# Two-layer graph network on one core: 96-row node tiles, x loads at the head of layer 1, node maximum from PSUM in two banks

## The reference

```python
def _leaky(x): return jnp.where(x >= 0, x, 0.01 * x)

def _edge_conv(x, src, dst, W1, b1, W2, b2):
    x_i, x_j = x[dst], x[src]
    h = jnp.concatenate([x_i, x_j - x_i], axis=-1)
    m = _leaky(h @ W1 + b1) @ W2 + b2
    return jax.ops.segment_sum(m, dst, num_segments=50000)

h = jnp.maximum(_layernorm(x), 0.0)
for l in range(2):
    h = _edge_conv(h, src, dst, W1[l], b1[l], W2[l], b2[l])
    h = _leaky(_layer_norm(h, g[l], b[l]))
return x + h
```

## Time and profile before

| | us |
|---|---|
| median of 3 runs | 1081.89 (1065.54 to 1090.26) |
| the profiled execution, its own time | 1051.49 |
| its span, first to last instruction | 1049.8 |
| DVE busy | 816.5 |
| PE busy | 848.6 |
| POOL busy | 727.7 |
| ACT busy | 591.7 |

### The profile page before, as it was taken

The page is one execution under the profiler, slowest core; times in us unless marked ns, Lnnn a source line. Parts: engine busy times, 40 slices in busy tenths (PEclk is TensorE's granted clock), DMA queues, the critical chain, the costliest instruction groups (busy, mean ns, idle before and its releaser), DMA issues.

```text
span 1049.8 us, 21951 instructions
## 1 busy us (share of the span) xinstructions
PE 848.6 (81%) x5756; PEld 691.8 (66%) x5756; DVE 816.5 (78%) x2330; ACT 591.7 (56%) x1632; POOL 727.7 (69%) x705
## 2 busy tenths in 40 slices
PE   1577788898889898988998647998888888888864
PEld 1345676777777677766777545777777777777753
DVE  6675687787887788787876313799999999999984
ACT  0145787888888788887888410433434343343431
POOL 4877777777777777777730007788888888888544
PEclk9998899999999999999999855999999999999965
DMA  1232477888687778776875551699999999999996
GB/s 38 77 81 76 109 173 190 210 201 212 182 211 190 203 193 214 193 203 179 199 183 133 145 151 49 149 246 276 272 272 265 270 270 259 276 267 266 256 265 174
DMA packets 338395, 204.11 MB, mean 194 GB/s; under 512 B 32986, under 2 KB 322589, under 8 KB 338269
## 3 DMA queue, kind: packets, MB, share of 16 engines
q1 hardware_dynamic: 190397, 99.95, 38.6%
q10 hardware_dynamic: 129056, 64.16, 22.2%
q0 software_dynamic: 18816, 38.57, 14.2%
HBM read 124.92 MB, written 77.62 MB: 193 GB/s over the span
## 4 chain that ended last, share of the span: by engine, by line
POOL 32%; DVE 23%; issue 21%; PE 8%; DMA 7%; ACT 4%; SPq 3%; DVEq 0%; ACTq 0%; POOLq 0%
POOL e_x L583 18%; POOL e_x L576 14%; DVE e_hT L856 5%; DVE e_n L856 5%; PE psum L902 3%; DVE e_same L750 3%; DMA e_x<-in_x,src_cols 3%; DVE e_rows L866 3%; DVE e_hidT L877 2%; SPq L531 2%; DMA b_rows<-e_rows 2%; DVE w_rel L735 1%; DMA h_rows<-w_out 1%; ACT e_n L633 1%; DVE n_stats L799 1%
## 5 line engine op out<-in xcount | busy, mean ns | idle before, releaser
L583 POOL DMA_INDIRECT e_x<-h_rows,src_cols x196 | 197.4, 1007 | 148.0 <-DMA h_rows<-w_out 93.9
L902 PE MATMUL psum<-w_win,w_oh 113*128 113x128 f32 x1568 | 227.0, 291 | 36.0 <-ACT w_out L613 21.7
L583 POOL DMA_INDIRECT e_x<-in_x,src_cols x196 | 205.9, 1051 | 59.8 <-issue 59.5
L576 POOL DMA_INDIRECT e_x<-in_x,dst_idx x196 | 194.2, 991 | 73.1 <-issue 58.2
L902 PEld LDWEIGHTS psum<-w_win,w_oh 113*128 113x128 f32 x1568 | 206.9, 205 | 42.2 <-issue 31.5
L618 ACT ACTIVATE e_v<-psum 128x512 f32<-128x512 f32 x98 | 59.4, 606 | 218.2 <-DVE e_hT L856 96.7
L910 PE MATMUL psum<-e_same,e_m 128*128 128x136 f32 (+2 forms) x1168 | 169.7, 290 | 0.0
L910 PEld LDWEIGHTS psum<-e_same,e_m 128*128 128x128 f32 x1168 | 149.3, 197 | 23.2 <-issue 21.2
L738 DVE TENSOR_TENSOR w_oh<-node_iota,w_rel 112x512 f32<-112x512 f32 x196 | 142.1, 725 | 6.7
L799 DVE BATCH_NORM_STATS2 n_stats<-e_x 128x6 f32<-128x128 f32 x392 | 80.4, 278 | 70.2 <-DMA e_x<-in_x,src_cols 69.1
L633 ACT ACTIVATE e_n<-e_x,n_shift,n_inv 128x128 f32<-128x128 f32 x196 | 80.5, 490 | 0.7 <-DVE n_shift L833 0.5
(11 more groups left out here) (164 smaller groups left out, 1677.9 us busy)
## 6 DMA issues: line engine op xcount, KB each, us to landing
w_win<-b_rows SPq DMA_DIRECT2D x784, 56.4 KB
h_rows<-w_out SPq DMA_DIRECT2D x98, 256.0 KB
e_line<-dst_lines SPq DMA_DIRECT2D x49, 288.0 KB
b_rows<-e_rows SPq DMA_DIRECT2D x49, 258.0 KB
b_rows<-e_rows ACTq DMA_DIRECT2D x49, 258.0 KB
e_x<-in_x ACTq DMA_DIRECT2D x49, 256.0 KB, 5.0
out<-e_x ACTq DMA_DIRECT2D x49, 256.0 KB
w_out<-in_x ACTq DMA_DIRECT2D x36, 256.0 KB, 4.8
```

Source lines behind the costliest of these rows:

```text
L576: pool.indirect_dma_start(e_x[:, slot, 0, k, :], None, table, bass.IndirectOffsetOnAxis(dst_idx[:, g * K + k:g * K + k + 1], 0)).then_inc( ...
L583: pool.indirect_dma_start(e_x[:, slot, 1, k, :], None, table, bass.IndirectOffsetOnAxis(src_cols[:, g * K + k:g * K + k + 1], 0)).then_inc ...
L902: last = nc.tensor.matmul(b_p[:, j, :], w_oh[0:W + 1, w % RH, j, :], w_win[0:W + 1, w % RW, j, 0:D], start=True, stop=True)
```

## The change

There are four edits. `W` becomes 96. The placements of layer 1 go into two banks in turn, `b_p` and `b_f` (`b_f` was used in layer 0 only), and wait for the maximum of the window before the last (`nodes_made`) and no longer for ACT's copy of the last one. ACT multiplies by the slope as it copies, and DVE takes the maximum of the PSUM bank and this copy. The first eight x loads are issued before step 0 of layer 1, and no longer in its steps 7 to 10.

```diff
-W = 112
+W = 96
@@
+        def place_bank(l, w):
+
+            return b_f if l == 1 and w % 2 == 1 else b_p
@@ raise_nodes (ACT)
-                nc.scalar.activation(e_v[:, w % 2, :], flat(b_p), ACT.Copy).then_inc(nodes_sloped, 1)
+                nc.scalar.activation(e_v[:, w % 2, :], flat(place_bank(1, w)), ACT.Copy, scale=SLOPE).then_inc(nodes_sloped, 1)
@@ layer 1 of ACT
+            for w in range(RQ):
+                load_x(w)
             for s in range(STEPS[1] + 1):
...
                 for w in windows(s - R1 - 3):
-                    load_x(w)
+                    if w >= RQ:
+                        load_x(w)
@@ leaky_nodes (DVE)
-                p_all = e_v[:, w % 2, :].rearrange("p (k d) -> p k d", k=K)
-                nc.vector.scalar_tensor_tensor(t_ring[w % RT], p_all, SLOPE, p_all, ALU.mult, ALU.max).then_inc(nodes_made, 1)
+                nc.vector.tensor_tensor(t_ring[w % RT], place_bank(1, w)[:, :, :], e_v[:, w % 2, :].rearrange("p (k d) -> p k d", k=K),
+                                        ALU.max).then_inc(nodes_made, 1)
@@ place (PE)
                 else:
-                    need(pe, nodes_sloped, w)
+                    pe.wait_ge(nodes_made, NODE_GROUPS + max(w - 1, 0))
                     if w == 0:
-                        pe.wait_ge(nodes_made, NODE_GROUPS)
+                        pe.wait_ge(rows_made[0], GROUPS)
+                        pe.wait_ge(scaled, GROUPS)
                         pe.wait_ge(const_out, 32)
                 for j in range(K):
-                    last = nc.tensor.matmul(b_p[:, j, :], w_oh[0:W + 1, w % RH, j, :], w_win[0:W + 1, w % RW, j, 0:D], start=True,
+                    last = nc.tensor.matmul(place_bank(l, w)[:, j, :], w_oh[0:W + 1, w % RH, j, :], w_win[0:W + 1, w % RW, j, 0:D], start=True,
                                             stop=True)
```

## The result

| | before | after |
|---|---|---|
| median of 20 runs on one chip, us | 1065.6 (1044.7 to 1090.3) | 1076.9 (1058.4 to 1093.7) |
| ratio, 95% interval | | 1.0179 [1.0129, 1.0229] |
| the profiled execution, us | 1051.5 | 1059.8 |

The changed kernel is slower by 1.8%. I had forecast 0.7% faster, so the sign is wrong. The ratio compares undisturbed runs only, which for a kernel with four or six runs can be a few long ones; over all 20 runs the medians lie 1.1% apart.

What follows compares the result with a forecast made beforehand. POOL was taken to limit layer 1's steady part (7.62 of a 7.65 us step). Terms -2 - 2.5 - 3.5 + 1 - 0.5 = -7.5 us gave 1044 against the profiled 1051.5, or 1074 for the median; range 1066 to 1081, with rivals and spread 1050 to 1094.

Steps and rivals of the forecast that it cites:

- The steady part: Layer 1's 37 steps up to the last gathers: POOL stays the limit, 2 us gained; ends 11 gained and 22 lost.
- 0.05 of the 0.30: First gather of each steady step: of its 0.30 us stretch, 0.05 was expected to go, 2 us in all.
- The mechanism of the stretch: POOL's gathers: one that begins while a DVE instruction with two SBUF operands runs takes 1.24 us, not 0.94.
- The base: Steady part of layer 1: the kernel before takes 7.65 us a step, read from one profile.
- The new wait: PE's placement waiting for DVE's maximum: closes a loop of 7.0 us, below POOL's 7.62, so costed at nothing.
- After the last gather: End of layer 1: 2.5 us saved as maxima stop waiting behind adds, 3.5 saved in the last windows.
- my 4.95: Last windows of layer 1: two windows take about 4.95 us in place of 5.65, saving 3.5 us in all.
- The x loads: Between layer 0's last store and POOL's first gather: early loads delay it by 1 us, between 0 and 4.
- W (-0.5): Window transfers carry 1/7 less: 0.5 us saved where layer ends wait for windows; ends 0 and 4.
- a gain in layer 0: Sign of being wrong: layer 0 getting faster; no size given.
- The rival of the DMA limit: Steady part: DMA engines were the limit, so fewer bytes save 0.24 us a step, 9 in all; chance 0.05.
- The slower rival: Steady part: the new wait's loop, with L862 behind one POOL add, becomes 8.25 us a step, +22 us; chance 0.10.

Runs made afterwards that it cites:

- e8: Kernel before with the node numbers that L738 compares copied to a free PSUM bank, leaving it one SBUF operand; 1081.1 us, ratio 1.0162.
- e2: e1 with the placement again waiting for ACT's copy, so two banks, W = 96 and early x loads stay on the changed kernel; 1072.0 us.
- e3: Kernel before with W = 96 in place of 112 alone; 1071.9 us, ratio 1.0025.
- e4: Kernel before with the eight x loads issued ahead of layer 1 alone; 1081.8 us, ratio 1.0315.
- second profile of before: Kernel before, unchanged, run and profiled again; 1076.3 us, ratio 1.0011.
- e15: Kernel before with 17 extra products on PE at the head of layer 1; 1084.5 us, ratio 1.0297.
- e17: e15 with one push: in one step of 49, POOL's adds wait for DVE's maxima of the next pair of windows; 1065.2 us, ratio 1.0050.
- e1: Changed kernel with the old maximum, taken on DVE from the SBUF copy; 1086.8 us.
- second profile of after: Changed kernel, unchanged, run and profiled again; 1078.0 us, ratio 1.013.
- e11: Changed kernel with the first eight x loads back in steps 7 to 10; 1067.5 us, ratio 1.0142.
- e9: Changed kernel with PE's first placement of a step moved behind the message product and ACT's copy of it behind the squares; 1087.3 us, ratio 1.0130.
- e12: Changed kernel with the matmul that clears the sum's bank run three times ahead of the placement, in place of once; 1078.2 us, ratio 1.0139.
- e18: Changed kernel with one push: in one step of 49, POOL's adds wait for DVE's maxima of the next pair of windows; 1076.8 us, ratio 1.0194.
- e7: Kernel before with only the maximum from PSUM and the two banks with their new wait; W = 112, x loads in the steps; 1073.9 us, ratio 1.0104.
- e14: Kernel before with the x add of every second window moved from POOL to DVE; 1055.2 us, ratio 0.9966.
- e10: Changed kernel with the x add of every second window moved from POOL to DVE; 1053.1 us, ratio 0.9966.
- e13: e10 with 17 extra products on PE at the head of layer 1; 1055.7 us, ratio 0.9953.
- e16: Kernel before with one push: in one step of 49, POOL's adds wait for DVE's maxima of the next pair of windows; 1062.3 us, ratio 1.0082.

## Why the prediction was wrong, point by point

*The steady part (forecast -2, measured +7.8 in the profiles).* The step that failed is: "L882 has two SBUF operands, so it waits for their end and is running when the first gather begins, as the old maximum was. I take 0.05 of the 0.30". That came true in the early steps, but I followed DVE to the first gather and no further. Behind the old maximum, the second gather at 803.54 met L877, which has an operand in PSUM, and L882 began 0.10 after it; behind L882 stand L750 and then L738 (L745 now), which begins 0.9 us after L882's end, just ahead of the second gather, and costs another 0.33. Where L742 takes the place, L745 follows at once and costs 0.50 on the first. The value for this term should have been a range of both signs, from -0.30 to +0.33 a step; my upper end came from the loop alone. The mechanism of the stretch, read from the gather at 676.66, was right, and e8 shows it.

The Trainium skill (SBUF — State Buffer, Who interferes with whom) says that a DVE instruction with two SBUF inputs contends with GpSimd's reads, and infers of `tensor_tensor` that it takes only the read side of the shared pair, while descriptor generation needs the write side. For these indirect gathers the runs show that it does hold them up: gathers of 0.94 take 1.27 and 1.43 when one begins under the `tensor_tensor` L745, and the one at 803.49 is back at 0.94 with the operand in PSUM. The gathers also read their row numbers from SBUF (`src_cols`). Whether that read is what waits, which would agree with the page's rule on reads, no run here separates.

*The base.* I took 7.65 for the kernel's own step. The same kernel also runs at 8.20 (1088 us, of which 13 come from the head of layer 1) and, with the loads or 17 products at the head, at 8.06 and 8.20 almost throughout. The profiled execution of before was among its fastest. Comparing the orders, the change saves 0.2 a step in two of them and loses the third. That is shown for the profiles, not counted over the timed runs, of which only the sums are known. From 7.65 to 7.86 or 7.98 is 8 to 12 us over 37 steps. With the 1.4 of the x loads and the 3.3 after the last gather, and less the 3.9 of layer 0 (below), that is an estimate of 9 to 13 us, 0.8 to 1.2%: as far apart as the medians are (1.1%), and less than the ratio of 1.8%, whose rest is not shown.

*The new wait (costed at nothing, cover 0.6).* At the upper clock that holds: POOL has no gap before its adds in the profiled execution. What I left out is the lower level, where PE's own work in a step is 12 us and no cover is left. In the profiles with POOL's adds as they were, the long steps come mostly with the new wait. Over 9 us there are none of the 37 in before, e2, e3, e4 and e8, and, pushes aside, one or two at the very start of the steady part in the second profile of before, in e15 and in e17. There are 4 in e1, 5 in the second profile of after, 5 in e11, 12 in e9, 2 in e12, one in e18. e1 and e2 differ in that wait alone, with 312.8 against 297.8 us for the 37 steps. Against it speak the first profile of after and e7, with the new wait and none, although the clock lay at its lower level for 13.7 and 27.3 us of their steady parts. With the x add split, e14 has the old wait and four such steps, of 9.3, and e10 and e13 have the new one and 2 and 8. These are single profiles: the wait is a hint and not shown as a cause. Why the clock falls there is open; filling a part of the gap did not stop it.

*After the last gather (forecast -6, measured +3.3).* Of the loss, 2.9 is there at once. Behind the adds that follow the last gathers, the next pair of windows gets its first add 6.0 us later (986.46 behind 980.42), where it was 3.1 before (978.61 behind 975.47): in the order of 7.65 its maxima were already running behind those adds (976.42). At the very end the gain of the two banks did not come either. DVE's rows of the changed kernel:

```profile
1025.75 0.85 DVE L742 TENSOR_SCALAR w_rel<-w_win,group_neg 96x4 f32<-96x4 f32 x1
1026.63 1.72 DVE L745 TENSOR_TENSOR w_oh<-node_iota,w_rel 96x512 f32<-96x512 f32 x1
1030.12 0.23 DVE L742 TENSOR_SCALAR w_rel<-w_win,group_neg 96x4 f32<-96x4 f32 x1 [1.77 <-DMA w_win<-b_rows]
...
1035.59 0.23 DVE L742 TENSOR_SCALAR w_rel<-w_win,group_neg 96x4 f32<-96x4 f32 x1 [0.80 <-PE psum L910]
```

L742 and L745 stand behind the adds, 1.7 us together, but they did so before as well (L735 1.23 in place of 0.22, and L738 1.71 in place of 0.69 at 1019.92). What is new in these last windows is that DVE then waits: 1.77 and later 1.47 for windows, and 0.80 for PE. PE's two placements run as one block of 3.75 and then wait 1.7 to 2.7 for the maximum. Two windows take 4.6 to 6.45 (1025.37 to 1031.82: 6.45), against my 4.95. I had named late windows and the stalled L735 as "late next" and then taken a value near the floor. I had also let the chain overlap with itself. At 1035.59 it does not: L742 needs a slot that the second placement of the pair frees, and behind that placement come one matrix (0.9) and the first maximum (0.7) before the next placement can begin. With my 4.1 for two placements that is 5.7 and no longer 4.95; the pair took 5.46 with its block of 3.75.

*The x loads (+1)* were right in sign and near in size. From ACT's last copy of layer 0 to POOL's first gather there are 3.64 to 3.67 us in every profile with the loads in the steps (before twice, e3, e7, e8, e11, e14, e15, e16, e17) and 4.95 to 5.45 in every one with the loads at the head (after twice, e1, e2, e4, e9, e10, e12, e13, e18). That is 1.3 to 1.8 us, 1.4 in the two profiles of the result. e4's other loss came with its order; taken out of the change, in e11, the loads moved no more than that: the ratio stayed 1.014.

*W (-0.5)* holds for the times: e3 is at 1.0025. But a gain in layer 0 was one of my signs of being wrong, and there is one. The last copy of layer 0 begins at 617.5 to 626.6 in the eleven profiles with 96 rows and at 621.8 to 629.9 in the nine with 112, with means of 622.1 and 626.0. I had looked at layer 1 alone; which wait became shorter is open. The rival of the DMA limit falls with it, since the share went to 0.90 with longer steps. The slower rival named the wrong trigger (L862 behind an add); its loop through PE, ACT and DVE shows itself in the long steps at the lower clock, and not in the steps of 7.86 and 7.98, where POOL has no gap.

What happened in the steady part is a rival that I did not have: the stall moves from an instruction that does little harm to one that does more.

## What to carry to other kernels

An instruction that stands behind another engine's lock is not only waste; it also holds its engine's order in place. Before you remove such a stall, look for the next instructions that would take it, and follow them over all of the other engine's transfers, not the first alone. Where two engines chase each other in a loop, one profile shows one order of several: take a second profile of the unchanged kernel, or push one step, before you price a change in tenths of a step.

## What the runs showed of the hardware

- A gather of POOL (0.94 us) that begins while DVE runs a 128x512 instruction with two operands in SBUF took 1.14 to 1.47 (1.14 at 803.65 in e4, 1.24 at 715.93, 1.43 at 810.16, 1.47 at 805.98 in e8), the more the more of that instruction was left; with one of the two operands in PSUM it took 0.94.
- The same instructions in the same order on every engine ran steps of 7.65 (before), 8.06 (e4) or 8.20 us (the second profile of before) for some 300 us on end. One changed wait moved 8.20 to 7.65 in e17, and in e2 the steps of 7.65 ended where DVE waited 0.59 us for a window.
- From the first gather of layer 1 to the first add, the unchanged kernel took 61.2 us at a mean granted clock of 0.80 and 74.4 us at 0.50.
- TensorE's granted clock stood at 0.50 for 12 us amid the steady part (715 to 727), with PE busy for the whole of it, and was back to 0.94 in the next 13 us.
- More work on PE at the head of layer 1 made no higher clock there: 0.50 from 640 to 680 in e13 and in e15 all the same.
